# Input tiles of a block-quantised MLP turned over DRAM and VectorE instead of TensorE

## The reference

```
xn  = layernorm(x)                                   # per token
ssm = state-space scan over time of rmsnorm(xn), 16 states a feature
a   = xn + ssm;  a = a + gelu(rmsnorm(a)*scale2 @ w1 + b1) @ w2 + b2        # 512 -> 2048 -> 512
q(t) = blockwise FP4 quantise and dequantise, blocks of 16 along the last dimension
h   = silu(q(xn) @ q(w_gate).T) * (q(xn) @ q(w_up).T)                       # 512 -> 1408
out = x + a + q(h) @ q(w_down).T                                            # 1408 -> 512
```

## Time and profile before

| what | us |
|---|---|
| median of three runs | 3289.08 (3286.53 to 3289.84) |
| the profiled execution | 3286.65, of it span 3284.9 |
| TensorE products busy | 3140.0 (96% of the span), 15340 instructions |
| VectorE busy | 1962.9 (60%) |
| ScalarE busy | 1085.5 (33%) |
| GpSimd busy | 1074.8 (33%) |

### The profile page before, as it was taken

How to read it: one execution, slowest core, us unless ns; L and a number is a source line. 1 busy time by engine, 2 the same in 40 slices (tenths; PEclk the granted TensorE clock), 3 DMA queues, 4 the chain that set the end, 5 groups by cost and what they waited for, 6 DMA issues and landing times.

```text
span 3284.9 us, 43359 instructions
## 1 busy us (share of the span) xinstructions
PE 3140.0 (96%) x15340; PEld 2530.9 (77%) x15340; DVE 1962.9 (60%) x4369; ACT 1085.5 (33%) x1908; POOL 1074.8 (33%) x1037
## 2 busy tenths in 40 slices
PE   5789899999998999999999999999999999999999
PEld 3577777778876777777777788888888888888887
DVE  7788788887775666666677654444444444444442
ACT  5335555544443333333332322112221212122211
POOL 7545455555453444444444311101111110111100
PEclk9999999999999999999999999999999999999999
DMA  4121222226654455455543422222222222222210
GB/s 118 42 62 59 89 89 62 88 70 163 164 157 102 132 148 145 130 151 137 130 117 78 125 52 42 52 38 50 52 48 49 48 47 52 42 52 42 52 20 26
DMA packets 594855, 272.65 MB, mean 83 GB/s; under 512 B 425040, under 2 KB 516432, under 8 KB 592080
## 3 DMA queue, kind: packets, MB, share of 16 engines
q1 hardware_dynamic: 594640, 269.88, 33.1%
HBM read 193.75 MB, written 76.05 MB: 82 GB/s over the span
## 4 chain that ended last, share of the span: by engine, by line
PE 61%; DVE 19%; POOL 7%; issue 6%; ACT 3%; DMA 1%; SPq 1%; DVEq 0%; ACTq 0%; POOLq 0%
PE bank L831 21%; PE bank L815 21%; PE bank L687 9%; PE bank L709 4%; POOL qa L1450 4%; DVE qs L937 3%; POOL qa L1456 3%; DVE qa L954 3%; DVE qa L909 2%; DVE qb L962 2%; DVE sg L901 2%; DVE qs L948 2%; PE bank L751 2%; PE bank L659 1%; DVE qs L942 1%
## 5 line engine op out<-in xcount | busy, mean ns | idle before, releaser
L815 PE MATMUL bank<-hT,Wp 128*128 128x512 f32 x3072 | 749.4, 393 | 1.4 <-ACT gf L1401 1.3
L831 PE MATMUL bank<-Wp,G 128*128 128x512 f32 x3072 | 743.5, 391 | 0.0
L831 PEld LDWEIGHTS bank<-Wp,G 128*128 128x128 f32 x3072 | 576.7, 188 | 125.6
L815 PEld LDWEIGHTS bank<-hT,Wp 128*128 128x128 f32 x3072 | 572.2, 188 | 122.8 <-ACT gf L1401 1.8
L687 PE MATMUL bank<-XT,Wg 128*128 128x512 f32 (+1 forms) x2148 | 532.4, 397 | 28.3 <-DVE XT L969 15.0
L1152 DVE CAST G<-gf 128x512 fp32r<-128x512 f32 x256 | 110.4, 431 | 749.5 <-PE bank L831 748.2
L709 PE MATMUL bank<-Wd,HT 128*128 128x512 f32 x2112 | 527.6, 399 | 12.3 <-POOL HT L1464 12.3
L687 PE MATMUL bank<-XT,Wu 128*128 128x512 f32 (+1 forms) x2148 | 516.6, 390 | 22.4 <-DVE sg L901 22.4
L687 PEld LDWEIGHTS bank<-XT,Wg 128*128 128x128 f32 x2148 | 400.3, 192 | 127.5 <-DVE XT L969 24.1
L687 PEld LDWEIGHTS bank<-XT,Wu 128*128 128x128 f32 x2148 | 403.1, 191 | 111.0 <-issue 29.9
L709 PEld LDWEIGHTS bank<-Wd,HT 128*128 128x128 f32 x2112 | 395.4, 191 | 106.2 <-POOL HT L1464 13.3
(11 more groups left out here) (111 smaller groups left out, 2838.3 us busy)
## 6 DMA issues: line engine op xcount, KB each, us to landing
px<-in_L_attn_x_dram SPq DMA_DIRECT2D x128, 256.0 KB, 2.9
xin<-in_L_attn_x_dram SPq DMA_DIRECT2D x128, 256.0 KB, 3.7
sT<-r_K SPq DMA_DIRECT2D x128, 256.0 KB, 4.2
r_Z<-xin SPq DMA_DIRECT2D x64, 256.0 KB, 2.2
r_U<-ub SPq DMA_DIRECT2D x16, 1024.0 KB, 6.6
sU<-r_U SPq DMA_DIRECT2D x32, 512.0 KB, 5.0
r_Y<-sY SPq DMA_DIRECT2D x16, 1024.0 KB, 5.7
xl<-in_L_attn_x_dram SPq DMA_DIRECT2D x64, 256.0 KB, 3.0
```

The source lines that it names most:

```text
L815: ins = e.matmul(bk[:], Wp[f][wh][:, 0, k * P:(k + 1) * P], hT[xh][b % 2][:, k, :], start=(k == 0 and p_ == 0), stop=(k == KD - 1 and p_ = ...
L831: ins = e.matmul(ACC[j][:], G2[gh][:, n % 2, j * P:(j + 1) * P], Wp[f][wh][:, 1, :], start=(f == 0 and p_ == 0), stop=(f == 15 and p_ == 2))
```

## The change

Input tiles outside the head (60 of 64: x4 to x63) are no longer turned by TensorE. SP stores the dequantised tile in DRAM (`r_X`, two slots) in window s + 1, and in window s + 2 reads it back into the tile's `xin` buffer in four transfers, one for each quarter of 32 features, in runs of 32 elements, so that one block transpose of 32 by 32 on VectorE (`x_turn`, window s + 3, in the place of `low`) gives the whole turned tile. It is written to `XW`, which has the memory of XT1, the buffer of the rest; ScalarE copies the high part from it to XT0 (`x_high`), and GpSimd subtracts in place (`x_low`). One more weight tile goes through the head (33 jobs), side jobs stand in other windows, with their loads issued three windows behind the tile that had the buffer before, each tap stage's stores stand ahead of the other DMAs of their window, and up to six instead of three small steps of the batched square root run in a window below 14. The turns that are left outside the head (five weight tiles) all use bank GB.

```
-HEAD = ([("w", i) for i in range(14)] + [("x", 0), ("x", 1)] + [("w", i) for i in range(14, 28)]
+HEAD = ([("w", i) for i in range(14)] + [("x", 0), ("x", 1)] + [("w", i) for i in range(14, 29)]
...
-SIDE = {w - 27: ("w", w) for w in range(28, 34)}
-SIDE.update({7: ("x", 4), 8: ("x", 5), NF - 1: ("x", 6), NF: ("x", 7)})
-SIDE.update({NF * i + o: ("x", 4 * i + j) for i in range(2, NB) for o, j in ((-7, 0), (-4, 1), (-2, 2), (-1, 3))})
+SIDE = {1: ("w", 29), 2: ("w", 30), 3: ("w", 31), 4: ("w", 32), 5: ("x", 4), 6: ("w", 33), 7: ("x", 5), 8: ("x", 6),
+        10: ("x", 7)}
+SIDE.update({NF * i + o: ("x", 4 * i + j) for i in range(2, NB) for o, j in ((-9, 0), (-7, 1), (-3, 2), (-2, 3))})
+PLACE = [q % 2 if q < 6 else (q + 1) % 2 for q in range(len(SIDES))]
+EARLIER = [max((p for p in range(q) if PLACE[p] == PLACE[q]), default=None) for q in range(len(SIDES))]
...
-TAPS = [s for s in range(K0, S0) if s - 2 not in SIDE][0:32]
+TAPS = [s for s in range(K0, S0) if s - 3 not in SIDE][0:32]
...
+            def tile_out(m):                                  # SP, window s + 1, behind px loads and u_out
+                n = XPOS[m]
+                e.wait_ge(s_ph, m + 1)
+                e.dma_start(r_X[n % 2], qa[:, m % 4]).then_inc(d_so[n % 2], 16)
+            def tile_back(m):                                 # SP, first in window s + 2
+                n = XPOS[m]
+                e.wait_ge(d_so[n % 2], 16 * ((n + 1) // 2))
+                e.wait_ge(s_pa, m + 1)
+                for q in range(4):
+                    e.dma_start(xin[32 * q:32 * q + 32, place(m)].rearrange("p (k r i) -> p k r i", k=KD, r=4),
+                                bass.AP(r_X.tensor, n % 2 * P * D + 32 * q, [[D, 32], [P, KD], [32 * D, 4], [1, 32]])
+                                ).then_inc(d_xb[place(m)], 16)
...
+                    if s == TAPS[2 * i + 1] + 2:              # SP, ahead of z_out, loads and px loads
+                        kernel_w_out(i)
+                    if i % 4 == 3 and s == TAPS[2 * i + 1] + 2:
+                        kernel_row(i // 4)
...
-                if s in SIDE and SIDES.index(SIDE[s]) + 1 < len(SIDES):
-                    side_load(SIDES.index(SIDE[s]) + 1)
+                for q, p in enumerate(EARLIER):
+                    if p is not None and s == SWIN[SIDES[p]] + (3 if SIDES[p][0] == "x" else 0):
+                        side_load(q)
...
-                if side(s - 2) is not None:
+                if side(s - 2) in TPOS:                       # TPOS: weight tiles and the head's tiles only
                     turn(side(s - 2))
...
+            def x_turn(m):                                    # VectorE, window s + 3
+                n = JOBS[m][1] // 2
+                e.wait_ge(d_xb[place(m)], 64 * returns(m))
+                if n >= 3:
+                    e.wait_ge(s_gu, last(n - 3) + 1)
+                e.transpose(whole(m), xin[:, place(m)].rearrange("p (k c) -> p k c", c=P)).then_inc(s_xt, 1)
...
+            def x_high(m):                                    # ScalarE, window s + 3, behind h_high
+                e.wait_ge(s_xt, XPOS[m])
+                e.activation(job_dst(m)[0], whole(m), ACT.Copy).then_inc(s_xh, 1)
...
+            def x_low(m):                                     # GpSimd, window s + 3, behind dequant(h)
+                hi, lo = job_dst(m)
+                e.wait_ge(s_xh, XPOS[m])
+                e.tensor_tensor(lo, whole(m), hi.bitcast(F32), ALU.subtract).then_inc(s_xlo, 1)
```

More of the change, by code:

```diff
@@ L205, in build @@
             Wu.append([sbt(actx, f"Wu{f}{h}", [P, KD, P], F32R) for h in range(2)])
-        XT = [sbt(actx, f"XT{h}", [P, 3, KD, 2 * P], F32R) for h in range(2)]
+        XT = [sbt(actx, "XT0", [P, 3, KD, 2 * P], F32R)]
+        with ExitStack() as wctx:
+            XW = sbt(wctx, "XW", [P, 3, KD, 2 * P])
+        XT.append(sbt(actx, "XT1", [P, 3, KD, 2 * P], F32R))
         xin = sbt(actx, "xin", [P, 4, 512])
@@ L335, in job_dst, with whole @@
             return [h[:, i // 2 % 3, :, i % 2 * P:(i % 2 + 1) * P] for h in XT]
+        def whole(m):
+            i = JOBS[m][1]
+            return XW[:, i // 2 % 3, :, i % 2 * P:(i % 2 + 1) * P]
         def inputs(h, w, k):
@@ L346, in turned, with place, loads, returns @@
         def turned(m):
[L347 to L352, removed]
+            return (bank[(5, 7)[TPOS[m] % 2]] if m < NJ else GB)[:, 0:job_width(m)]
+        def place(m):
+            return PLACE[SIDES.index(JOBS[m])]
+        def loads(m):
+            return PLACE[:SIDES.index(JOBS[m]) + 1].count(place(m))
+        def returns(m):
+            return sum(place(p) == place(m) for p in XTURNS[:XPOS[m]])
         def job_in(m):
@@ L357, in job_in @@
                 return qa[:, m % 4, 0:n]
-            return xin[:, m % 4 if m < NJ else SIDES.index(JOBS[m]) % 2, 0:n]
+            return xin[:, m % 4 if m < NJ else place(m), 0:n]
         def wait_qa(e, m):
@@ L549, in window @@
                 k = s - S0
+                if side(s - 2) in XPOS:
+                    tile_back(side(s - 2))
+                for i in range(16):
+                    if s == TAPS[2 * i + 1] + 2:
+                        kernel_w_out(i)
+                    if i % 4 == 3 and s == TAPS[2 * i + 1] + 2:
+                        kernel_row(i // 4)
+                    if i % 4 == 3 and s == TAPS[2 * i + 1] + 3:
+                        kernel_v_out(i // 4)
                 for n in range(NP):
@@ L609, in sync_program @@
             side_load(0)
+            side_load(1)
             for s in range(SW, NW + 1):
@@ L728, in ssm_states @@
                     e.wait_ge(s_q, MSSM)
-                    e.wait_ge(s_lo, max(TPOS[side(w)] for w in SIDE if w + 2 < S0 - 1))
                     e.wait_ge(s_kV, 16)
@@ L930, in biggest @@
                 elif JOBS[m][0] == "w":
-                    q = SIDES.index(JOBS[m])
-                    e.wait_ge(d_xs[q % 2], 16 * (q // 2 + 1))
+                    e.wait_ge(d_xs[place(m)], 16 * loads(m))
                 else:
@@ L1065, in window @@
                 h_mult(s - 1)
-                if low_x is not None:
+                if low_x in TPOS:
                     low(low_x)
+                elif low_x is not None:
+                    x_turn(low_x)
                 h_rows(s - 1)
@@ L1327, in window @@
                 k = s - S0
-                if side(s - 3) is not None:
+                if side(s - 3) in TPOS:
                     high(side(s - 3))
@@ L1331, in window @@
                     h_high(s - 2)
+                if side(s - 3) in XPOS:
+                    x_high(side(s - 3))
                 if h_job(s) is not None:
@@ L1506, in window @@
                 dequant(h)
+                if side(s - 3) in XPOS:
+                    x_low(side(s - 3))
                 j = tap_pair(s - 1)
```

61 lines of the change are left out of this document (31 added, 30 removed).

## The result

The changed kernel takes 3274.81 us (median of 5 runs, 3272.98 to 3276.91) where the kernel before takes 3289.08 (5 runs, 3286.53 to 3290.52). The ratio is 0.9958, with a 95% interval of 0.9943 to 0.9972: 14 us are won, and the forecast was 36.

The account below looks back on a forecast made before the run. TensorE was taken to bound the scan's stage, VectorE's chain the windows before 1040 us. Terms 0 - 11.7 - 9 + 8 - 3 - 20 = -35.7 us gave a 3253 us median; own range 3238 to 3266, stated range 3230 to 3282.

Parts of the forecast that it names:

- the cost of the returns, +8 us: Tiles read back from DRAM: seven behind r_U stores 1.2 us late each, +8 us, up to +25; ordinary tiles in time.
- the scan's stage, -20 us: 1040 to 1730 us: removing 24 turns from TensorE gives 11.3 us, plus 9 us of idle time; ends 8 and 29.
- I take 9 of them: Scan's stage: of TensorE's 14.4 us idle, 9 are recovered; some of it is VectorE's lateness, which stays.
- Before 1040 us the turns' TensorE time is worth nothing: Before the scan's stage: VectorE sets the pace, so taking the turns off TensorE wins 0 us there.
- The waits for the high part, 9.3 + 2.4, to count in full: 200 to 950 us: VectorE's removed waits for ScalarE's high part win 11.7 us where VectorE sets the pace.
- The taps' stores, -9: Around 354 us: moving the taps' stores forward removes GpSimd's wait for r_K, 9 us off, between 6 and 12.
- Head, 0 within 2: Head and side schedule: one more head job costs 2.9 us, the windows shed about 3; zero, within 2 either way.
- The start of the scan's stage, -3: Earlier loads remove a 5.6 us DMA wait there; 3 taken, because x38's return queues behind the scan's first loads.
- Everything is hidden: Rival, whole kernel: returns come in time and all idle time is won, 3234 us; chance 0.20.
- Serial reads: Rival, tile returns: the four reads go one behind another, costing 80 us before 1040 us, 3325 us; chance 0.08.
- `x_low` locks out VectorE: Rival, before 1040 us: GpSimd's x_low blocks VectorE through the shared port, 29 us given back, 3282 us; chance 0.06.
- The chain takes over in the scan's stage: Rival, scan's stage: VectorE and ScalarE become the bound, 5 us won instead of 20, 3268 us; chance 0.12.

Follow-up runs that it names:

- e1_parked: Changed kernel with x_turn reading a weight tile already in SBUF, so nothing waits for the return while all transfers still run: 3229.85 us, 0.9828.
- e2_order: Changed kernel with SP's 1 MB r_U stores issued one window later, behind the tile's return: 3262.44 us, 0.9924.
- e3_slot: Changed kernel with x_turn moved behind mid_b(h) in VectorE's window and x_high to the end of ScalarE's: 3227.65 us, 0.9821.
- e10_turns_kept: e3_slot with TensorE again turning each of the 60 tiles, its wait for silu included, and nobody reading the result: 3248.22 us, 0.9876.
- e4_schedule: Kernel before with only the new schedules (head, side places, taps' stores first, six steps a window), input tiles still turned by TensorE: 3270.88 us, 0.9952.
- e5_stores: Kernel before with only the taps' stores moved first in SP's window and kernel_row one window earlier: 3278.44 us, 0.9969.
- e8_low_twice: e3_slot with a second GpSimd instruction of x_low's size behind it in each of the 60 tiles: 3262.85 us, 0.9918.
- e7_plain: Changed kernel with the return as one DMA in runs of 2 KB instead of four in runs of 128 bytes: 3254.41 us, 0.9902.

## Why the prediction was right in direction and wrong in size

Without any cost of the returns the forecast's terms add to -46.3 us (-35.7, less the 8 behind `r_U` and the 2.6 kept back for the return of x38); e1_parked shows -57.2. With it they add to -35.7; the changed kernel shows -13.7. So two steps failed, in opposite senses, and the first weighs more. It is luck that the second took some of the first back: the forecast is 22 us off and would otherwise be further off.

*Step that failed: the cost of the returns, +8 us.* By e1_parked it is 43.5 us. It has three parts: 17 in windows 66 to 98, 6 at the start of the scan's stage, 21 in it.

Behind `r_U` the step said "With 1 MB in flight beside it I take 1.2 us late". The mechanism and the place were right: in windows 66 to 98 six of its seven tiles wait, 17.5 us in all, 2.9 each. (The seventh, x38, waits 6.0 us in window 99. That wait stays at 5.7 in e2_order, so it is not the 1 MB store that makes it late; its reads stand behind the scan's first loads, as the forecast said.) The forecast had the tile back 10.6 us after its store's issue (4.5 held, 2.2 to land, 3.9 for the reads) and wanted 10.9 after. Measured are 12.6 and 9.3 in the one place and 12.1 and 9.3 in the other: the store lands up to 1.5 us later than held time and landing add to, the reads take 0.6 to 1.2 us more because four issues take 2.60 us and not 1.5, and `x_turn` comes 1.6 us sooner. The sum stayed below its upper bound of 25; the longest single wait, 4.3, passed the 3.5 that a tile was given. e2_order takes away the cause alone and wins 16.5 us in that stretch.

In the scan's stage the step said that waits of a few us for some twelve tiles are "hidden". There are 14, of 3.3 us, about as forecast, and they are not hidden: 21 us. The argument was that VectorE had waited 5.0 us there before while TensorE stayed at 98%. It overlooked that the scan stands behind `x_turn` in VectorE's order and that TensorE's `ssm_outputs` need the scan in the same window, 16.0 us on L797, and it had no term for the clock that falls around the longest of these waits, some 5 us. An engine at 98% does not show that a wait elsewhere is free; it shows that 2% is what such waits cost so far. The reckoning gave 12 x 3 = 36 us for "if it were not", and that term belonged in the forecast at about half.

*Step that failed: the scan's stage, -20 us.* With the waits gone it is -35.7 (e1_parked) or -36.8 (e3_slot), beyond the upper end of 29. The turns were sized well, 0.57 us each by e10_turns_kept against 0.47. Too small was the idle time recovered, "I take 9 of them": TensorE's idle time in windows 101 to 166 fell from 16.2 us to 0.2, so nothing of it stayed. e4_schedule shows that some of it, 5.6 us, comes with the new places alone. Turns, 13.7, and idle time, 16.0, make 30. Of the other 7 some 1.7 are, by estimate, the clock: in the kernel before it is 0.50 for 3.41 us behind a turn's wait for `silu` of 2.28 us, and in e3_slot it is full all through the stage. The rest is open.

```profile
1143.51:1146.92 3.41, 3.41 (x30) 3.08 (x30) 2.89 (x4) 0.00 (x0) 2.16 (x3) 0.50 0.00 0
```

*"Before 1040 us the turns' TensorE time is worth nothing"* is wrong by 10 us in e10_turns_kept, where each idle turn waits for `silu` (30.9 us before 1040) and holds the next gate products. How much of that is the turn and how much the wait was not separated.

*The waits for the high part, 9.3 + 2.4, to count in full:* windows 28 to 66 lost 6.4 us, and 6.5 of this wait lay there. That the two agree does not show the rule: e5_stores keeps the turn and loses 3.1 us in the same windows, and in e4_schedule the wait there is twice as long, 13.4 us, while the windows are 0.6 us shorter than before. Windows 66 to 98 without the lateness show -0.8 to -1.4 of 2.4 (e2_order, e1_parked).

*The taps' stores, -9:* right, -8.3 alone and -7.5 in the change.

*Head, 0 within 2:* it is 2.6 us longer, e4_schedule has the same 2.8, so the schedules are the cause.

*The start of the scan's stage, -3:* -4.5, and -10.5 without the return of x38. Both directions of the argument held, and the sizes were about double: the return cost 6.0 and not 2.6, and the schedule alone gives -9.2 (e4_schedule) and not -5.6. The stages of the earlier trace rows leave out 950 to 1040, where a single wait of 7.7 us for the high part stood; with the new places it is 0.3, the turn still on TensorE.

*The rivals.* "Everything is hidden", 3234, is what e1_parked and e3_slot show to be there, and more. "Serial reads" did not happen: ordinary tiles before 1040 us came in time, with no wait of `x_turn` between windows 14 and 66. "`x_low` locks out VectorE" is small in the changed kernel: in windows 2 to 98 VectorE is busy for 703.2 us against 698.7 before. It is 715.8 in e3_slot, which is the fastest but one all the same, and e8_low_twice shows how near the limit is. "The chain takes over in the scan's stage" fell with e3_slot. The lock and the serial reads were priced over 28 tiles before 1040 us; there are 36 (x4 to x39), which makes them 37 us instead of 29 and some 92 instead of 80. Neither was what happened.

## What to carry to other kernels

Price a wait by what stands behind it on its own engine and who needs that in the same window, not by how busy the bounding engine is. An instruction whose input comes by a long way round belongs at the end of its engine's window; here moving two calls was worth 44 to 47 us, more than three times the change itself. When work is moved off the bounding engine, run the new schedule with the work left where it was: only that shows which of the two paid.

## What the hardware showed that was not expected

A DMA issued behind a store of 1 MB on the same queue pays twice: its issue is held 4.5 us and it lands up to 8.2 us after issue began, where the same 256 KB take 2.1 (median) otherwise. Three waits of 2.5 to 4.9 us on a TensorE that is otherwise busy all the time ended in 3.41 us at half its clock in the changed kernel's scan stage; in e2_order waits of 2.3 and 3.1 us there did not. The time that SP takes to issue depends on the shape: 0.32 to 0.35 us for the tile in runs of 2 KB (e7_plain), 0.64 for a quarter of it in runs of 128 bytes, at most 1.5 (medians and longest of the changed kernel).
